# Five engine orders of a fused RWKV-style block, written out anew

## What is computed

```
xn  = layernorm(x);  sx = shift(xn)                      # previous token minus this one
t   = tanh((xn + sx*maa_x) @ maa_w1)                     # five small mixes of 32
x5  = xn + sx * (maa_stack + t @ maa_w2)                 # five mixed inputs: w, k, v, r, g
w   = exp(-exp(time_decay + tanh(x5_w @ decay_w1) @ decay_w2))
r,k,v = x5_r @ Wr.T, x5_k @ Wk.T, x5_v @ Wv.T;  g = silu(x5_g @ Wg.T)
scan over tokens, 32 heads of 8x8:  a = k v^T;  out = r (u*a + s);  s = a + w*s
x   = x + (groupnorm(out)*gn_w + gn_b) * g @ Wo.T
xn2 = layernorm(x);  xk, xr = two shifted mixes of xn2
x   = x + sigmoid(xr @ ffn_Wr.T) * (relu(xk @ ffn_Wk.T)^2 @ ffn_Wv.T)
```

## Time and profile before

| | |
|---|---|
| three timed runs | 522.01, 521.29, 521.96 us; median 521.96 |
| span of the profiled execution, first to last instruction | 520.3 us |
| time around the span | the page gives the profiled execution no time but its span; against the timed runs 0.9 to 1.7 us lie around it, 1.6 against the median |
| PE busy | 479.2 us (92%) |
| DVE busy | 474.4 us (91%) |
| ACT, POOL busy | 281.7 us (54%), 101.6 us (20%) |

### The profile page before, as it was taken

The page is one execution under the profiler, slowest core; times in us unless marked ns, Lnnn a source line. Parts: engine busy times, 40 slices in busy tenths (PEclk is TensorE's granted clock), DMA queues, the critical chain, the costliest instruction groups (busy, mean ns, idle before and its releaser), DMA issues. The chain is left out here.

```text
span 520.3 us, 6254 instructions
## 1 busy us (share of the span) xinstructions
PE 479.2 (92%) x2200; PEld 284.2 (55%) x2200; DVE 474.4 (91%) x528; ACT 281.7 (54%) x612; POOL 101.6 (20%) x93
## 2 busy tenths in 40 slices
...
DVE  2688899979999999999999989999999999999765
...
DMA packets 26999, 69.49 MB, mean 134 GB/s; under 512 B 1624, under 2 KB 19928, under 8 KB 24536
## 3 DMA queue, kind: packets, MB, share of 16 engines
...
## 5 line engine op out<-in xcount | busy, mean ns | idle before, releaser
L630 DVE TENSOR_TENSOR_SCAN kv<-w_sb,kv 128x512 f32<-128x512 f32 (+2 forms) x144 | 146.6, 1084 | 0.1
L958 PE MATMUL pa<-x,large_sb 128*128 128x512 f32 (+2 forms) x272 | 115.2, 567 | 5.0 <-DVE x L545 2.9
L451 POOL COPY kv<-s_sb 128x32 f32<-128x32 f32 (+2 forms) x36 | 54.6, 1518 | 145.6 <-PE patt L1130 141.4
L958 PEld LDWEIGHTS pa<-x,large_sb 128*128 128x128 f32 x272 | 51.2, 194 | 57.5 <-issue 44.3
L620 DVE TENSOR_TENSOR kv<-vrep,k_sb 128x2016 f32<-128x2016 f32 (+2 forms) x34 | 70.1, 2064 | 3.3 <-issue 3.3
L638 DVE TENSOR_TENSOR kv<-kv,r_sb 128x2048 f32<-128x2048 f32 (+2 forms) x36 | 72.9, 2043 | 0.2
L536 DVE SCALAR_TENSOR_TENSOR x<-pb,vec_sb,sx 128x512 f32<-128x512 f32 (+1 forms) x64 | 42.7, 708 | 6.0 <-PE pb L1002 5.9
L420 POOL DMA_DIRECT2D x<-xn x21 | 20.0, 951 | 111.5 <-DVE x L536 111.5
L1130 PE MATMUL patt<-kv,const_sb 128*32 128x512 f32 (+2 forms) x288 | 34.7, 557 | 0.5 <-DVE kv L638 0.4
L1002 PE MATMUL pb<-th,w_sb 32*128 32x512 f32 (+2 forms) x100 | 33.3, 596 | 1.5 <-DVE x L536 1.5
L1156 PE MATMUL pc<-large_sb,att 128*128 128x256 f32 x120 | 32.0, 390 | 0.0
...
## 6 DMA issues: line engine op xcount, KB each, us to landing
vrep<-v_scratch SPq DMA_DIRECT2D x12, 2048.0 KB, 18.5
x<-xn POOLq DMA_DIRECT2D x18, 512.0 KB, 8.3
...
x_tok<-in_x SPq DMA_DIRECT2D x6, 512.0 KB, 10.2
...
xres<-in_x SPq DMA_DIRECT2D x6, 512.0 KB, 10.7
out<-xres SPq DMA_DIRECT2D x6, 512.0 KB, 5.0
out<-trr POOLq DMA_DIRECT2D x6, 512.0 KB, 8.1
```

What stands on the lines that cost most here:

```text
L451: pool.tensor_copy(kv[:, q % 2, :, 0:nb, 0], s0_sb[:, half, G4 * j:G4 * (j + 1), FIRST[c]:FIRST[c] + nb]).then_inc(s0_put, 1)
L630: ins = dve.tensor_tensor_scan(flat, w_sb[:, p, q % HF, 0:nb].rearrange("p b t -> p (b t)"), flat, 0.0, ALU.mult, ALU.add)
L958: ins = pe.matmul(dst[:, m, 0:n], w(a)[:, m * P:(m + 1) * P], src[:, a, :], start=(a == 0), stop=(a == HF - 1))
```

## The change

The five head, table and tail lists become five plain texts, one per engine, in which every step stands with its chunk (`X4.0` is X4 of chunk 0). The set of steps is the same; the order is new on all five engines. `WARM` is unchanged. One wait is added, on SP: `vl1` too waits for the stores of v, since it can now stand ahead of `vl0`.

```diff
-DVE_HEAD = [("st1", 0), ("nrm1", 0), ("shift", 0), ("mix2", 0), ("mix0", 0), ("cwv", 0), ("mix1", 0),
...
+DVE_STEPS = """
+    st1.0 nrm1.0 shift.0 cwv.0 mix0.0 mix2.0 mix1.0 mix3.0 cs0.0 a0.0 a1.0 rk.0 shift.1 mix4.0 sc0.0 sc1.0 rs0.0
+    rs1.0 bonus.0 mix0.1 mix1.1 a2.0 mix2.1 sc2.0 mix3.1 a3.0 sc3.0 mix4.1 rs2.0 rs3.0 rk.1 a0.1 bonus.1 shift.2
...
+PE_STEPS = """
+    T1.0 W1.0 X01.0 X2.0 X3.0 P0.0 D1.0 P1.0 D2.0 VS.0 P3.0 T1.1 X4.0 CB.0 P4.0 W1.1 X01.1 BO.0 S0.0 S1.0 P0.1
...
-LAGS = 6
...
-def schedule(head, table, tail):
-
-    return head + [(name, i - lag) for i in range(NCH + LAGS) for name, lag in table
-                   if 0 <= i - lag < NCH and (name, i - lag) not in head + tail] + tail
+def schedule(text):
+
+    return [(name, int(c)) for name, c in (step.split(".") for step in text.split())]
...
             def load_v(c, p, half):
-                if half == 0:
-                    sp.wait_ge(v_stored, 16 * JH * (c + 1))
+                sp.wait_ge(v_stored, 16 * JH * (c + 1))
```

More of the change, by code:

```diff
@@ L32 @@
 NQ = JH * HF
[L35 to L46, removed]
-SUBS = 3
[L48 to L63, removed]
-DVE_HEAD = [("st1", 0), ("nrm1", 0), ("shift", 0), ("mix2", 0), ("mix0", 0), ("cwv", 0), ("mix1", 0),
[6 rows of a table removed]
-            ("out", 0), ("shift", 3), ("bonus", 2), ("sc0", 2), ("gate", 1), ("rs0", 2), ("mix0", 3),
-            ("mix1", 3)]
@@ L73 @@
-PE_HEAD = [("T1", 0), ("W1", 0), ("X01", 0), ("X2", 0), ("X3", 0), ("D1", 0), ("D2", 0), ("P0", 0), ("P1", 0),
[6 rows of a table removed]
-ACT_HEAD = [("st", 0), ("nrm", 0), ("xn", 0), ("th", 0), ("thd", 0), ("st", 1), ("v", 0), ("w", 0), ("nrm", 1),
[5 rows of a table removed]
-POOL_HEAD = [("ad4", 0), ("ad0", 0), ("rd1", 0), ("rd1", 1), ("ad1", 0), ("s00", 0), ("s01", 0), ("ad3", 0),
[3 rows of a table removed]
-SP_HEAD = [("vst", 0), ("lx", 0), ("lr", 0), ("lx", 1), ("lx", 2), ("lx", 3), ("vl0", 0), ("vl1", 0),
-           ("vst", 1), ("vl0", 1), ("vl1", 1), ("sx2", 0), ("lx", 4), ("vst", 2), ("lr", 1)]
+SUBS = 3
```

58 lines of the change are left out of this document (53 added, 5 removed), and 20 rows, old and new, of tables (ACT_HEAD, DVE_HEAD, PE_HEAD, POOL_HEAD).

## The result

The changed kernel takes 537.55 us (median of 534.18, 534.63, 540.47 and 541.22) against 521.99 of the kernel before on the same chip: ratio 1.0295, 95% interval 1.026 to 1.0329. It is 15.6 us slower where 6.2 less was forecast, and outside the range. The profiled execution took 540.47 us, with a span of 538.7; it is one of the two longer ones. Its mean granted clock is 0.971, which over its span is 15.6 us lost to the clock, where the two shorter ones (534.18 and 534.63) lost 10.1, so what the profile shows is rather more than a typical execution has. Since the kernel before moved a little from one series to the next (520.75 to 523.04), kernels of different series are compared by their ratios; 0.001 of ratio is 0.52 us.

What follows compares the result with a forecast made beforehand. DVE's queue, 98% busy in the middle, was taken to set the pace. Terms -5.5, -2.0, -1.7, +1.0, +1.0, +1.0 gave -6.2: span 520.3 to 514.1, time 515.7 us; range 510.5 to 524.5.

Steps and rivals of the forecast that it cites:

- The start: Centering of Wv and mix0 first, X4 ahead of CB, BO behind X01: 5.5 us gained, bounds 2 and 6.8.
- the centering with mix0 first: DVE in chunk 0: centering of Wv fills a wait and mix0 goes first, 2.3 us gained, bounds 0 and 2.3.
- P0 of chunk 1: PE at the start: the transfer chain to a0 of chunk 1 moves as P0 moves, 5.8 us earlier.
- Chunk 2: Load of v with only lx between store and load: a0's 2.72 us wait shrinks, 2.0 gained, bounds 0 and 2.7.
- The clock dip: PE's half clock near 299 us doesn't come, so DVE gets back 1.7 us; bounds 0 and 1.7.
- Rival D: Clock dips come in every round, seven at 1.7 us: +7.4, 529.4 us; chance 0.04.
- v behind nrm2: ACT in middle rounds: v ends some 3.9 us later, leaving its chain no slack; 1.0 us lost in all.
- rival C: Chain from v to the loads becomes the bound at a0 of chunks 3 to 8: +12.4, 534.4 us; chance 0.19.
- ad4 of chunk 6: POOL: its DMA waits for S2 of chunk 5, so P4 waits and mix0 is delayed; 1.0 us lost.
- The rest: Other middle-round moves, such as shift2, CB and short waits for X steps: 1.0 us lost, bounds -3 and +4.
- An order can win only idle time of DVE: Whole kernel: DVE's work stays the same, so gains are limited to idle 20.9, 10.3 and 14.7 us.

Runs made afterwards that it cites:

- e5_head: The kernel before with only the start's edits on DVE, PE and ACT: 518.73 us, ratio 0.9939.
- e17_newq_lx5: e10_newq with lx.5 put behind the load vl0.2 on SP: 523.57 us, ratio 1.0007.
- e10_newq: e5_head with the new SP and POOL queue orders, as mended in e4_three: 527.56 us, ratio 1.0103.
- e4_three: The changed kernel with ad4 of chunks 6 and 8, lx.8 and shift.2 all moved earlier: 533.25 us, ratio 1.0223.
- e7_v: e4_three with the copy of v ahead of nrm2 on ACT in chunks 2 to 8, as before: 531.25 us, ratio 1.0167.
- e1_ad4: The changed kernel with ad4 of chunks 6 and 8 moved earlier on POOL, as before: 536.19 us, ratio 1.0258.
- e2_lx8: The changed kernel with the load of x for chunk 8 ahead of the stores of v of chunk 7 on SP: 533.43 us, ratio 1.0192.

## Why the prediction was wrong

- **The start, forecast -5.5: right in mechanism and place, too large.** mix0 of chunk 1 stood at 41.55 (forecast near 41), X4 was no longer waited for, a0 of chunk 1 stood at 65.6 (near 64). a0.1 was 3.9 earlier; e5_head gives -3.2 in the time. Two terms were mis-sized: the centering with mix0 first gave 1.2 of 2.3 by a0 of chunk 0 (27.41 against 28.64), and P0 of chunk 1 came 4.4 earlier (45.18 against 49.57), not 5.8. From P0 on the transfer chain moved as was said: the load of v of chunk 1 went out 4.4 earlier too (55.54 against 59.93). Missed was what stood there: DVE arrived 5.4 earlier, so a0 waited 2.02 instead of 0.55, and shift of chunk 2 stood behind that wait and `bonus`.
- **Chunk 2, forecast -2.0: wrong in sign.** a0.2 waits 4.54, not 0.7. The step that failed was to take the steps between store and load as what held the load up, and the removal of lr as the gain. With lr between them the load went out 10.9 us behind the stores, and with nothing between them (e17_newq_lx5) 11.0 behind: the stores' own time sets it, and nothing was to be won. What was lost in the changed kernel is 1.0 from store to load, with lx.5 between, and 1.8 because the stores came later. That lx.5 has a wait of its own, for the buffer it overwrites, was overlooked; it held nothing up here, but in e10_newq it held the load back for 4.5 us, and e17_newq_lx5 prices it at 5.0 us of the time.
- **The clock dip, forecast -1.7: wrong in sign.** In place of one dip behind 60 us there are five in the profile. Rival D had 0.04. It was put as dips from short waits alike in both orders; what came were, four times of five, dips behind new waits of 2 to 4 us on PE. Its sum also charges the dip that the kernel before has already. The rule of the Trainium skill, "TensorE: Matmul & The Clock Gate", section "A second HAM failure mode: psum-queue depth-cycling", fits, of those five, the one at 304 us alone, where PE's largest wait ahead was 0.89; at the four stretches quoted above it was a long pause.
- **v behind nrm2, forecast +1.0, and rival C (0.19): not what happened.** In the changed kernel the waits for loaded v of over 2 us are at chunks 1 and 2, in e4_three at 2 and 6, and in neither in every round; e7_v leaves the second in place and takes 1.5 us off the first. Its gain of 2.9 us isn't beyond the uncertainty, so a cost of the size of the forecast 1.0 is neither shown nor excluded.
- **ad4 of chunk 6, forecast +1.0: right place, too small.** Landing took 14.2, P4 waited 3.37, its matmuls took 5.40 instead of 3.60, and DVE waited 5.33. The forecast took DVE to arrive "about as late"; it didn't, and the half clock wasn't counted. Mended by itself (e1_ad4) it gives 3.1 us between the gates of chunks 5 and 6.
- **The rest, forecast +1.0 with a bound of 4: here the largest of the three late steps was missed.** lx.8 behind the stores of v of chunk 7 made st.8 late, and rr.5 and KK with it: 5.4 us (e2_lx8), with an uncertainty of 3.4. The bound had been set from short waits for X steps, and the order of SP against ACT's `st` was never walked through.
- **One reasoning error ran through all.** "An order can win only idle time of DVE" was used for what can be won, 46 us in the whole span. What can be lost has no such bound. A middle with 10.3 us idle in 420 had nothing to give, and five queues were laid out anew against each other there; each edge between them was a chance to lose. Pricing the seen edges at about 1 each and the unseen at 1 together was the fault. How the loss is shared among the steps of the computing engines stays open.
